# Mixer and MoE block on one core: Y's norm moved ahead of the result's statistics on VectorE, and sixteen repeated products on TensorE before the last group's Y

## The chip, the core and the metric

The kernel runs on one core of a Trainium2 chip. The core's engines each work through a program of their own and meet only at semaphores: TensorE (PE in the profile, its weight loads PEld) multiplies, VectorE (DVE), ScalarE (ACT) and GpSimd (POOL) work elementwise, and SyncE (SP) issues the transfers. Products land in PSUM, which is eight banks here, `bank[0]` to `bank[7]`, of 512 columns each. The metric is the device time of one execution in microseconds (us); lower is better. TensorE's clock has two levels, 1.2 and 2.4 GHz; the profile gives the granted clock of a stretch as a share of the upper one.

## What is computed

An input x of 8 sequences of 1024 tokens with 128 features goes through a recurrent mixer with four heads, a residual sum and a norm; the result, called Y in the kernel, goes through a mixture of experts (16 experts, the best 4 of each token, and a shared one), a residual sum and a norm again:

```python
x = _layernorm(x + mixer(x, ...), axis=-1)            # Y in the kernel
x = _layernorm(x + moe(x, ...), axis=-1)              # z2, then the output

def _layernorm(x, axis=-1, eps=1e-05):
    m = jnp.mean(x, axis=axis, keepdims=True)
    v = jnp.var(x, axis=axis, keepdims=True)
    return (x - m) / jnp.sqrt(v + eps)

# moe, on all tokens xf:
g = sigmoid(xf @ gate_w.T)
topv, topi = top_k(g, 4);  wn = topv / sum(topv);  combine = scatter of wn
h = silu(xf @ e_win) * (xf @ e_vin) * combine          # per expert
out = sum over experts of h @ e_wout  +  silu(xf @ ws_in) * (xf @ vs_in) @ ws_out
```

## The kernel before

A first phase (to about 134 us in the trace) projects, convolves and computes the gates of all tokens and leaves what the mixer needs in DRAM. The second phase is the one that matters here. It goes over 16 groups g of 512 tokens (NG = 16, four chunks of 128 tokens each), and pairs the mixer of group g with the expert part of group f = g - 1, so that every engine's program alternates between the two. `groups` (line 319) sets this: `mix(0, None)`, then a loop over g = 1 to 14 with `mix(g, g - 1)`, then `mix(15, 14)`, and at the end `ffn(15)`, the expert part of the last group alone. The order on each engine is written out by hand; no scheduler changes it.

On TensorE, `mix(g, f)` (line 1410) begins with the transposes of Y (`ffn_head`, line 1348, which wait for `Y_done`), then the key transposes (`key_tokens`, line 1293, which wait for `val_out[1]`, VectorE's copy of the values), the routing logits (line 1354) and eleven slots j. A slot holds six products of 512 columns (`ffn_in`, lines 1366 to 1370: twice hi by hi, lo by hi and hi by lo parts, into `bank[4]` and `bank[5]`), a row product (line 1385), the output products (line 1395) and, in some slots, pieces of the mixer: the chunks of the recurrence (`chunk`, lines 1313 to 1320; chunk k waits for `state_done[k - 1]`), the head transposes (line 1329) and the down projection (line 1339). Last comes `mix_front(g + 1)`: keys, values and scores of the next group (lines 1258, 1267, 1284).

VectorE's `mix(g, f)` (line 1020) ends with what this change touches. `mixer_out` adds the residual (line 1008, `y1`) and takes the statistics of y1 (lines 990 to 998). `ffn_sum` adds the expert output in `bank[7]` to the Y of group f, which is `z2` (line 1105), and takes the statistics of z2. `mixer_norm` writes the new Y over the old one (line 1002), once GpSimd has made `rs1`, the reciprocal root, by one power operation (`power`, line 552). Then come `mix_front(g + 1)` (the values, line 925, and two score products, line 934), `yT_low` (line 1046), and `ffn_norm` (line 1002 again, this time z2 into `out_sb`, which waits for `rs2`). In the next round VectorE goes on with the keys (line 940), the routing (lines 1055 to 1086), the product h of slot 0 (line 1097), and the two sums of `state` after chunk 0 (line 951).

GpSimd makes `rs1`, then `rs2` (line 552 both), and after these, for the next group, `kept` (line 567) and `mixed` (line 573, x times the skip weights, 512 columns from SBUF into SBUF). Later it computes the score masks `D` from `max_b` (line 538), which SyncE loads. SyncE's queue holds, in this order for each group: the store of `out_sb` (line 475, after `out_done`), `x_res`, then the loads of `max_b` (line 404), `xT2` and `inter_w` of the next group.

ScalarE copies the transposed Y out of `bank[7]` twice (`yT` and `yT_hi`, through the helper on line 619), takes the exponential of the logits (line 743) and the silu of each slot (line 754).

The statistics (line 988) are three steps, and each waits for the one before:

```python
for k in range(NC): i = dve.bn_stats(st[:, k], src[:, k])        # line 990
for k in range(NC): i = dve.bn_aggr(mv[:, k], st[:, k])          # line 995
dve.tensor_scalar(ve[:], mv[:, :, 1], EPS_LN, None, ALU.add)     # line 998
```

## Time and profile before

| | us |
|---|---|
| median of 3 runs (lowest, highest) | 866.17 (864.02, 871.2) |
| the profiled execution: its own time | 864.57 |
| its span, first to last instruction | 862.8 |
| mean granted TensorE clock in it | 0.963 |

| engine | busy us | share of the span |
|---|---|---|
| PE | 787.7 | 91% |
| PEld | 666.1 | 77% |
| DVE | 644.4 | 75% |
| ACT | 363.7 | 42% |
| POOL | 371.7 | 43% |

1.8 us of the execution's time lie around the span. The sixteen sums y1 begin between 170.9 and 816.8 us, so one group takes 43.06 us on average; the last expert part alone takes the time from 822 us to the end. Busy shares are averages over the whole span; a matmul's end is modelled, so that the distance between the starts of two of them is the better measure of what one costs. In the timelines a row can hold several instructions of one kind (x4), with the time from the first's start to the last's end; brackets hold the idle time of the engine before the row and what ended it.

### The profile page before, as it was taken

Reading aid. Unit: us, or ns where it says so; the run is one execution under the profiler, and the core shown is the slowest. Engines: PE = TensorE matmul, PEld = TensorE weight load, DVE = VectorE, ACT = ScalarE, POOL = GpSimd, SP = SyncE. Lnnn points to the kernel's source line nnn. Section 1 sums busy time; section 2 is a strip of 40 time slices with the busy share of each in tenths; the row PEclk is TensorE's granted clock in tenths of the full one; section 3 lists DMA queues with packets and bytes.
Section 4 is the critical chain, followed back from the end, with each engine's and each line's share of the span. In section 5 each row is a group of like instructions: output and inputs, shape, how many; then the busy total and the mean of one; then the engine's idle time right before and its main releaser. Section 6 shows DMA issues by size and latency. Waiting matters only on the chain.

```text
span 862.8 us, 17647 instructions
## 1 busy us (share of the span) xinstructions
PE 787.7 (91%) x5783; PEld 666.1 (77%) x5783; DVE 644.4 (75%) x1711; ACT 363.7 (42%) x621; POOL 371.7 (43%) x370
## 2 busy tenths in 40 slices
PE   6888968689999999999999999999999999999976
PEld 5656656578888888888888798888898888888855
DVE  5799953377778777777777877777878777778754
ACT  4757833143434343434343434343434343434131
POOL 5050008553455455454545544545455454543200
PEclk8999977599999999999999999999999999999979
DMA  4887744030404040404040405040404040400000
GB/s 121 237 259 262 288 177 127 30 123 25 135 24 134 24 134 24 134 24 134 24 132 26 134 24 132 26 133 25 134 24 134 24 134 24 134 24 25 1 13 13
DMA packets 53104, 81.01 MB, mean 94 GB/s; under 512 B 10176, under 2 KB 36952, under 8 KB 49112
## 3 DMA queue, kind: packets, MB, share of 16 engines
q1 hardware_dynamic: 53080, 80.68, 30.4%
q8 instruction: 16, 0.26, 0.1%
q14 instruction: 8, 0.07, 0.0%
HBM read 55.24 MB, written 25.43 MB: 93 GB/s over the span
## 4 chain that ended last, share of the span: by engine, by line
PE 45%; DVE 19%; issue 15%; DMA 9%; POOL 6%; ACT 2%; SPq 2%; POOLq 1%; DVEq 1%; ACTq 0%
PE bank L1395 11%; DMA max_b<-max_scratch 8%; PE bank L1366 5%; PE bank L1370 5%; PE bank L1367 5%; DVE acc L838 5%; PE bank L1339 3%; DVE st L990 3%; PE bank L1315 3%; PE bank L1385 3%; PE bank L1313 2%; PE bank L1320 2%; DVE Y L1002 2%; POOL D L548 2%; POOL D L538 2%
## 5 line engine op out<-in xcount | busy, mean ns | idle before, releaser
L754 ACT ACTIVATE s_in<-bank 128x512 f32<-128x512 f32 x144 | 86.1, 598 | 175.9 <-PE bank L1370 174.8
L1395 PEld LDWEIGHTS bank<-ewout,h 128*128 128x128 f32 x1024 | 132.8, 191 | 8.5
L1366 PE MATMUL bank<-yT_hi,in_hi 128*128 128x512 f32 x288 | 128.0, 444 | 8.3 <-DVE h L1097 8.3
L1395 PE MATMUL bank<-ewout,h 128*128 128x128 f32 x1024 | 134.9, 275 | 0.0
L1097 DVE TENSOR_TENSOR h<-s_in,bank 128x512 f32<-128x512 f32 x144 | 98.2, 682 | 49.0 <-PE bank L1370 42.2
L552 POOL TENSOR_TENSOR rs<-ve,half 128x4 f32<-128x4 f32 x32 | 32.6, 1019 | 206.6 <-DVE ve L998 206.6
L1370 PE MATMUL bank<-yT_lo,in_hi 128*128 128x512 f32 x288 | 114.3, 397 | 0.0
L1367 PE MATMUL bank<-yT_hi,in_lo 128*128 128x512 f32 x288 | 113.9, 395 | 0.0
L538 POOL TENSOR_TENSOR D<-a_tok,max_b 128x512 f32<-128x512 f32 x64 | 65.4, 1043 | 110.7 <-DVE max_b L910 67.8
L1101 DVE TENSOR_TENSOR h<-h,bank 128x512 f32<-128x512 f32 x128 | 87.2, 681 | 14.4 <-PE bank L1385 14.4
L951 DVE TENSOR_TENSOR state<-kept,bank 64x130 f32<-64x130 f32 x128 | 36.6, 286 | 59.1 <-PE bank L1320 29.6
L619 ACT ACTIVATE u_sb<-bank 128x260 f32<-128x260 f32 x64 | 24.8, 388 | 131.1 <-PE bank L1315 131.1
L567 POOL TENSOR_TENSOR kept<-state,decay 128x260 f32<-128x260 f32 x64 | 39.7, 620 | 89.0 <-DVE state L951 88.8
L1315 PE MATMUL bank<-vals,C 128*128 128x65 f32 x512 | 73.9, 269 | 0.0
L1366 PEld LDWEIGHTS bank<-yT_hi,in_hi 128*128 128x128 f32 x288 | 55.1, 191 | 20.9 <-DVE h L1097 15.2
L1315 PEld LDWEIGHTS bank<-vals,C 128*128 128x128 f32 x512 | 70.5, 199 | 0.0
L580 POOL TENSOR_TENSOR r_h<-var_h,half 128x8 f32<-128x8 f32 x32 | 52.9, 1653 | 40.2 <-DVE var_h L971 39.1
L838 DVE SCALAR_TENSOR_TENSOR acc<-xm,vecs,acc 128x512 f32<-128x512 f32 x96 | 68.2, 780 | 0.0
L1370 PEld LDWEIGHTS bank<-yT_lo,in_hi 128*128 128x128 f32 x288 | 54.6, 190 | 12.9
L1313 PE MATMUL bank<-state,qs 128*128 128x130 f32 x256 | 56.6, 304 | 7.5 <-issue 5.2
L1367 PEld LDWEIGHTS bank<-yT_hi,in_lo 128*128 128x128 f32 x288 | 55.4, 192 | 5.3
L1313 PEld LDWEIGHTS bank<-state,qs 128*128 128x128 f32 x256 | 41.2, 197 | 16.5 <-issue 15.3
(193 smaller groups left out, 1623.6 us busy)
## 6 DMA issues: line engine op xcount, KB each, us to landing
xact_scratch<-xact SPq DMA_DIRECT2D x16, 1024.0 KB, 4.8
max_b<-max_scratch SPq DMA_DIRECT2D x15, 1024.0 KB, 7.8
xa<-xact_scratch SPq DMA_DIRECT2D x16, 512.0 KB, 6.2
silu_z<-xact_scratch SPq DMA_DIRECT2D x16, 512.0 KB, 3.8
inter_w<-inter_scratch SPq DMA_DIRECT2D x30, 256.0 KB, 7.1
x_in<-in_L_attn_x_dram SPq DMA_DIRECT2D x16, 256.0 KB, 4.8
xt_scratch<-x_t SPq DMA_DIRECT2D x16, 256.0 KB, 4.9
xT<-xt_scratch SPq DMA_DIRECT2D x16, 256.0 KB, 8.2
```

Source lines behind the costliest of these rows:

```text
L538: pool.tensor_tensor(D[:, kp, par], a_g.rearrange("p k (s two) -> p two k s", two=2)[:, par, 2 * kp:2 * kp + 2] .unsqueeze(3).to_broadcast ...
L580: pool.tensor_tensor(r_h[:, c].rearrange("p k h -> p (k h)"), var_h[:, c].rearrange("p k h -> p (k h)"), half[:, 0:2 * NH], ALU.pow).then_ ...
L754: act.activation(s_in[:, j % 2], bank[4][:], ACT.Silu).then_inc(silu_done, 1)
L838: i = dve.scalar_tensor_tensor(a, src, vecs[:, p, t:t + 1], a, ALU.mult, ALU.add)
L1097: dve.tensor_tensor(dst[:, j % 2], s_in[:, j % 2], bank[5][:], ALU.mult).then_inc(h1_done, 1)
L1101: dve.tensor_tensor(h2[:, (j - 1) % 2], h1[:, (j - 1) % 2], bank[6][:], ALU.mult).then_inc(h2_done, 1)
L1313: pe.matmul(o, qs[:, p, c], state[:, p], start=True, stop=False, skip_group_check=True)
L1315: i = pe.matmul(o[:, par * DV:(par + 1) * DV], C[:, par, kk, p], vals[:, k, 2 * p + par], start=False, stop=True, skip_group_check=True)
L1366: pe.matmul(o, in_hi[:, m, j], yT_hi[:], start=True, stop=False)
L1367: pe.matmul(o, in_lo[:, m, j], yT_hi[:], start=False, stop=False)
L1370: pe.matmul(o, in_hi[:, m, j], yT_lo[:], start=False, stop=True).then_inc(done, 1)
L1395: i = pe.matmul(bank[7][:, k * P:(k + 1) * P], h2[:, j % 2, k * P:(k + 1) * P], w, start=(j == k == 0), stop=(j == NJ), skip_group_check=True)
```

## The change

VectorE: `ffn_sum` keeps only the sum z2; its statistics are now `ffn_statistics`, called behind `mixer_norm`. `mixer_norm` waits for the sum z2 as well, since it overwrites the Y that the sum reads. `ffn(15)` calls both parts one after the other, as before. TensorE: `ffn`, which runs once, for the last group, begins with `stay_warm`, which waits for the last silu of the group before and issues 16 products of 512 columns into `bank[4]`; `ffn_in` of slot 0 overwrites them.

```diff
             def mixer_norm(g):
                 dve.wait_ge(rs1_done, g + 1)
+                dve.wait_ge(z2_done, g + 1)
                 normalise(Y, y1, mv1, rs1, Y_done)
@@ VectorE's mix(g, f)
                 mixer_norm(g)
+                if f is not None:
+                    ffn_statistics(f)
                 if not (isinstance(g, int) and g == NG - 1):
                     mix_front(g + 1)
@@
             def ffn_sum(f):
                 dve.wait_ge(o_mm, f + 1)
                 dve.tensor_tensor(flat(z2), bank[7][:], flat(Y), ALU.add).then_inc(z2_done, 1)
+
+            def ffn_statistics(f):
                 dve.wait_ge(z2_done, f + 2)
                 statistics(f, z2, st2, mv2, ve2, st2_done, mv2_done, ve2_done)
@@ VectorE's ffn(f)
                 ffn_sum(f)
+                ffn_statistics(f)
                 ffn_norm(f)
@@ TensorE
+            def stay_warm(f):
+                pe.wait_ge(silu_done, (f + 1) * (NJ + 1))
+                for i in range(WARM):
+                    pe.matmul(bank[4][:], in_hi[:, 0, 0], yT_hi[:], start=True, stop=True)
+
             def ffn(f):
+                stay_warm(f - 1)
                 ffn_head(f)
@@
+WARM = 16
```

VectorE's program in the loop over g = 1 to 14, at the end of `mix(g, g - 1)`. Before:

```order
L998 TENSOR_SCALAR ve<-mv 128x4
L1105 TENSOR_TENSOR z<-bank,Y 128x512
L990 BN_STATS st<-z 128x6 x4
L995 BN_AGGR mv<-st 128x2 x4
L998 TENSOR_SCALAR ve<-mv 128x4
L1002 TENSOR_SCALAR Y<-y,mv,rs 128x128 x4
L924 REGISTER_ALU
L925 COPY vals<-bank 128x8x64
```

Of the change:

```order
L998 TENSOR_SCALAR ve<-mv 128x4
L1108 TENSOR_TENSOR z<-bank,Y 128x512
L1002 TENSOR_SCALAR Y<-y,mv,rs 128x128 x4
L990 BN_STATS st<-z 128x6 x4
L995 BN_AGGR mv<-st 128x2 x4
L998 TENSOR_SCALAR ve<-mv 128x4
L924 REGISTER_ALU
L925 COPY vals<-bank 128x8x64
```

The norm of Y stands ahead of the nine instructions of z2's statistics, and behind the sum z2 in both; the copy of the values follows both in either program.

TensorE's program where the last group's expert part begins, behind the last output products of `mix(15, 14)`. Before:

```order
L1385 MATMUL bank<-combT,pair_rows 128x512
L1395 MATMUL bank<-ewout,h 128x128 x4
L1339 MATMUL bank<-w_down,mixed 128x128 x4
L1395 MATMUL bank<-ewout,h 128x128 x4
L1348 MATMUL bank<-ident,Y 128x128 x4
L1354 MATMUL bank<-w_gate,yT 128x16 x4
```

Of the change, whose lines below 1013 are numbered a few higher:

```order
L1391 MATMUL bank<-combT,pair_rows 128x512
L1401 MATMUL bank<-ewout,h 128x128 x4
L1345 MATMUL bank<-w_down,mixed 128x128 x4
L1401 MATMUL bank<-ewout,h 128x128 x4
L1435 MATMUL bank<-yT_hi,in_hi 128x512 x16
L1354 MATMUL bank<-ident,Y 128x128 x4
L1360 MATMUL bank<-w_gate,yT 128x16 x4
```

Sixteen products stand between the last output products and the transposes of the last Y; nothing else moved on TensorE. The programs of ScalarE, GpSimd and SyncE are the same.

## Rows read from the trace of the kernel before

**Rows 1.** Timeline of PE where group 8 ends and 9 begins: start us, us, instruction, [idle before].
```profile
522.88 0.66 PE L1348 MATMUL bank<-ident,Y 128*128 128x128 f32 x4 [0.34 <-DVE Y L1002]
523.48 0.66 PE L1293 MATMUL bank<-ident,keyT 128*128 128x128 f32 x4
...
529.54 0.40 PE L1370 MATMUL bank<-yT_lo,in_hi 128*128 128x512 f32 x1
530.15 0.46 PE L1313 MATMUL bank<-state,qs 128*128 128x130 f32 x2 [0.21 <-issue]
```

**Rows 2.** Timeline of DVE at the same boundary.
```profile
517.14 0.69 DVE L1008 TENSOR_TENSOR y<-bank,x_res 128x512 f32<-128x512 f32 x1 [1.10 <-PE bank L1339]
517.87 0.87 DVE L990 BATCH_NORM_STATS2 st<-y 128x6 f32<-128x128 f32 x4
...
519.38 0.68 DVE L1105 TENSOR_TENSOR z<-bank,Y 128x512 f32<-128x512 f32 x1
520.10 0.87 DVE L990 BATCH_NORM_STATS2 st<-z 128x6 f32<-128x128 f32 x4
...
521.72 1.11 DVE L1002 TENSOR_SCALAR Y<-y,mv,rs 128x128 f32<-128x128 f32 x4
522.74 0.69 DVE L925 COPY vals<-bank 128x512 f32<-128x512 f32 x1
523.34 1.28 DVE L934 TENSOR_TENSOR C<-bank,D 128x512 f32<-128x512 f32 x2
524.69 0.69 DVE L1046 TENSOR_TENSOR yT_lo<-bank,yT_hi 128x512 fp32r<-128x512 f32 x1
525.30 1.11 DVE L1002 TENSOR_SCALAR out_sb<-z,mv,rs 128x128 f32<-128x128 f32 x4
...
529.47 0.58 DVE L951 TENSOR_TENSOR state<-kept,bank 64x130 f32<-64x130 f32 x2
```

**Rows 3.** Timeline of POOL, then of ACT, at the same boundary.
```profile
519.55 1.01 POOL L552 TENSOR_TENSOR rs<-ve,half 128x4 f32<-128x4 f32 x1 [9.39 <-DVE ve L998]
521.89 1.03 POOL L552 TENSOR_TENSOR rs<-ve,half 128x4 f32<-128x4 f32 x1 [1.33 <-DVE ve L998]
522.89 0.62 POOL L567 TENSOR_TENSOR kept<-state,decay 128x260 f32<-128x260 f32 x1
523.49 1.56 POOL L573 TENSOR_SCALAR mixed<-xa,vecs 128x512 f32<-128x512 f32 x1
...
524.07 0.59 ACT L619 ACTIVATE yT_hi<-bank 128x512 fp32r<-128x512 f32 x1
```

**Rows 4.** Timeline of POOL and DVE behind group 0, without an expert part.
```profile
174.28 0.62 POOL L567 TENSOR_TENSOR kept<-state,decay 128x260 f32<-128x260 f32 x1
174.88 1.57 POOL L573 TENSOR_SCALAR mixed<-xa,vecs 128x512 f32<-128x512 f32 x1
...
174.35 2.18 DVE L1002 TENSOR_SCALAR Y<-y,mv,rs 128x128 f32<-128x128 f32 x4 [1.12 <-POOL rs L552]
```

**Rows 5.** Timelines of SP and POOL: the store, and the masks that wait for max_b.
```profile
526.58 0.41 SPq L475 DMA_DIRECT2D out_dram<-out_sb  x1
...
535.86 2.04 POOL L538 TENSOR_TENSOR D<-a_tok,max_b 128x512 f32<-128x512 f32 x2 [3.40 <-DMA max_b<-max_scratch]
```

**Rows 6.** Timelines of PE, DVE and ACT at the start of the last expert part.
```profile
816.65 1.06 PE L1395 MATMUL bank<-ewout,h 128*128 128x128 f32 x8
822.57 1.12 PE L1348 MATMUL bank<-ident,Y 128*128 128x128 f32 x4 [4.87 <-DVE Y L1002]
...
833.12 1.03 PE L1376 MATMUL bank<-ident,comb 128*32 128x128 f32 x4 [2.29 <-DVE comb L1086]
...
829.12 0.69 DVE L1097 TENSOR_TENSOR h<-s_in,bank 128x512 f32<-128x512 f32 x1 [1.78 <-PE bank L1370]
...
826.30 0.22 ACT L743 ACTIVATE ge<-bank 128x64 f32<-128x64 f32 x1 [0.19 <-PE bank L1354]
...
827.84 0.60 ACT L754 ACTIVATE s_in<-bank 128x512 f32<-128x512 f32 x1
```

**Rows 7.** Busy time by stretch: window: its length, PE, PEld, DVE, ACT, POOL, PEclk, DMA.
```profile
820.00:822.00 2.00, 0.00 (x0) 0.00 (x0) 1.82 (x12) 0.00 (x0) 0.78 (x2) 1.00 0.00 0
822.00:824.00 2.00, 1.12 (x4) 0.72 (x4) 0.52 (x3) 0.28 (x1) 0.61 (x1) 0.62 0.00 0
...
834.00:836.00 2.00, 2.00 (x6) 1.60 (x6) 0.00 (x0) 1.12 (x2) 0.00 (x0) 0.50 0.00 0
```

## The prediction

> **What bounds the kernel now.** I read the timelines of all engines around one boundary between two groups, since the change moves VectorE's work there, and then the start of the last expert part, where TensorE's new products stand. The fifteen later boundaries repeat within a few hundredths of a microsecond, so one stands for the fourteen in the loop over g = 1 to 14.
>
> At the boundary the time first passes from TensorE to VectorE: the sum y1 starts at 517.14, after a wait of 1.10 us for the down projection [rows 2]. TensorE then has the next group's front to do and needs Y only at the end of it: it waits 0.34 us for Y, starts the transposes at 522.88, and is nearly dense until 529.54 [rows 1]. Its next product, chunk 1, starts at 530.15. Products of 512 columns start 0.23 us apart here when nothing waits, so it could have started at about 529.77; what it waited for is `state`, whose two sums on VectorE run from 529.47 to 530.05 [rows 1, 2]. So both paths meet at chunk 1, and VectorE's is the later one, by 0.38 us. That path has almost no idle time: from 517.14 to 530.05 each row of VectorE starts when the one ahead of it lets it [rows 2]. It is therefore VectorE's work and not TensorE's wait for Y that sets when chunk 1 starts, and with it the rest of the group, in which TensorE is mostly dense.
>
> A second chain leaves from the same place. The store of `out_sb` is issued at 526.58, right behind the norm into `out_sb` (525.30 plus 1.11), and the load of `max_b` is queued behind it; GpSimd waits 3.40 us for that load and starts the masks at 535.86 [rows 2, 5]. Whatever delays `out_sb` delays this as well, so that neither chain can take up a slip of the other.
>
> **The change, step by step, in the loop (14 times).**
>
> 1. *Y's norm.* The sum z2 keeps its place, from 519.38 to 520.06. The norm needs `rs1`, which GpSimd makes from 519.55 to 520.56 [rows 2, 3]. A norm that waited for `rs1` started some 0.04 us behind it [rows 4], so it starts at 520.60 in place of 521.72: Y comes 1.12 us earlier. TensorE's wait of 0.34 us for Y goes. It can't take more: it is still at its scores until 522.54. And the key transposes behind (523.48 now) wait for the copy of the values, which comes later, below.
>
> 2. *What VectorE loses.* Before, z2's statistics started at 520.10 and covered the time in which `rs1` was made. Now VectorE stands still from 520.06 to 520.60. Then the four norms take 1.02 us (521.72 to 522.74, start to start), and the statistics 1.51 (517.87 to 519.38, those of y1) to 1.62 (520.10 to 521.72, those of z2) [rows 2]. The copy of the values starts at 520.60 + 1.02 + 1.51 to 1.62 = 523.13 to 523.24 in place of 522.74: a slip of 0.45 us, give or take 0.05.
>
> 3. *Up to `out_sb`.* The two score products follow with 0.60 us each after the copy. `yT_lo` waited 0.14 us for ScalarE's `yT_hi`: the second score product was issued at about 523.95, the next could have started at 524.55, it started at 524.69, and `yT_hi` ended at 524.66 [rows 2, 3]. `yT_hi` comes 0.34 us earlier now, with the transposes. That takes 0.14 off the slip. The norm into `out_sb` starts 0.31 us late, at 525.61.
>
> 4. *GpSimd meets VectorE.* z2's statistics end later, so `rs2` starts at about 523.37 (the value copy's new start, less 0.08 for the overlap with the last statistics step, plus its 0.17 and a start 0.08 behind it) in place of 521.89. `kept` and `mixed` are queued behind `rs2` and slip with it by 1.48 us: `mixed` ran from 523.49 to 525.05, just clear of `out_sb` at 525.30, and now runs from 524.97 to 526.53 [rows 3]. The norm into `out_sb` lies in it for 526.53 - 525.61 = 0.92 us. Behind group 0 the trace shows the same pair together: four norms take 2.18 us while GpSimd runs `kept` and `mixed`, against the 1.11 of both norms at the later boundary [rows 2, 4]. That is 1.07 us lost in 2.10 us of overlap (174.35 to 176.45), 0.51 per us. So 0.92 us of overlap costs 0.47 us. The ends of this term: nothing, if the phase is lucky, and 0.92, if VectorE stands still for all of it.
>
> The Trainium skill has a rule for this pair (the page "SBUF — State Buffer", section "SBUF: two separate sides"): VectorE and GpSimd share one pair of ports, held by one of them for a whole instruction, and the loser "fully blocks". By it the term would be 0.92. The trace agrees that there is a collision but not with a full block, since under it the four norms behind group 0 could not all have ended 0.08 us behind `mixed`.
>
> Sum for one boundary: 0.31 + 0.47 = 0.78 us later at `state`. TensorE gets to chunk 1 later by that, as its own path has not slipped as far (the key transposes wait for the copy of the values, 523.9 in place of 523.48, and the transposes of Y ahead of them left 0.34 us earlier; I put it at 0.2 to 0.4 us, inside the 0.38 us in hand plus 0.78). `mixed` and `kept` themselves are needed only at 529.47, so their slip costs nothing but the collision. 14 x 0.78 = 10.9 us. Bounds: 14 x 0.31 = 4.3 and 14 x 1.23 = 17.2.
>
> **The change at the end (once).**
>
> 5. *Y.* TensorE stands still for 4.87 us before the last transposes at 822.57 [rows 6]. The norm moves forward by 1.12 us as above, and nothing else is behind it here: 1.1 us gained.
>
> 6. *The sixteen products.* TensorE's last output products started at 816.65 and ended at 817.71; sixteen at 0.23 us are 3.7 us, from about 817.6 to 821.3, and the transposes can start at 821.45. So they lie wholly in the wait, with 0.1 us to spare, and cost nothing; at 0.25 us each or more they would begin to push the transposes, by 0.3 us for each 0.02. In their place the engine was idle, and its granted clock was 1.00 until 822, then 0.62 on average over the next 2 us, that is, it fell to the lower level within them [rows 7]. The transposes took 1.12 us against 0.66 in the loop [rows 1, 6]. I expect it to stay up. The silu of slot 0 started at 827.84 behind `ge`, which had waited 0.19 for the logits; with 0.46 from the transposes and these 0.19 the silu comes 0.65 earlier and ends 5.22 us behind the transposes' start. The product h of slot 0 started at 829.12, 6.55 behind it, held by TensorE's slow products; now it follows the silu: 1.3 us gained. Everything of the routing is queued behind that h, up to the combine transposes (833.12) [rows 6].
>
> 7. *The second fall.* There the clock is low again (0.50 from 834 to 836) [rows 7], after a wait of 2.29 us [rows 6]. That wait remains, at about 2.4 us, so I count nothing. If the clock holds, up to about 3 us at the lower level become 1.5: at most 1.5 gained; if it falls sooner, as much is lost.
>
> Sum at the end: 1.1 + 1.3 = 2.4 us gained, from 1.0 to 3.9.
>
> **Net.** +10.9 - 2.4 = +8.5 us. On the profiled execution's own time that is 864.57 + 8.5 = 873.1; that execution lies 1.6 us under the median of the runs, from which the same sum gives 874.7. I say 874.
>
> **Rivals.**
>
> *A. No collision.* `out_sb` and `mixed` alternate without loss, as one norm of the pair can slip through where GpSimd isn't at the memory. Then 4.3 - 2.4 = +1.9: 868. For it: the score products and `yT_lo` run at their usual time beside `kept` and `mixed` [rows 2, 3]. Against it: the norm has already been caught once [rows 4].
>
> *B. A full block.* 17.2 - 2.4 = +14.8: 881. It is what the lock would do, worked from `mixed`'s new end at 526.53; the full 1.07 of group 0 per boundary would end at much the same place.
>
> *C. TensorE's path decides (faster).* If chunk 1 isn't held by `state` but by something on TensorE's own path, then Y's 0.34 us comes off each boundary: 14 x 0.34 = 4.8, and with the 2.4 at the end -7.2: 859. This holds only if VectorE has at least 0.78 us in hand between the copy of the values and `state`; the rows show no gap of that size, and a wait of 0.38 us on the other side [rows 1, 2].
>
> *D. The products don't hold the clock.* They are the same product sixteen times, and the clock falls at 822 anyway. Then only Y's 1.1 us remain at the end: 10.9 - 1.1 = +9.8: 875.5 to 876. Against it: the level was 1.00 for the whole loop, in which TensorE did nothing else than such products.
>
> **How the numbers follow.** The forecast (collision at half rate, clock held) gets 0.45 with a range of its own of 870 to 878; A 0.17, B 0.18, C 0.10, D 0.10. The predicted time is 874. From 864 to 881 leaves out most of C, and the upper part of B, together under 2 in 10. About 1% (8.7 us) is what a measurement of this kernel can tell from no change. Faster by more than that (under 857.5) needs C and a kind tail: 0.05. Slower by more (over 874.8) takes B, most of D and nearly half of the forecast: 0.43. Within 1%: 0.52.
>
> **What would show it.** In the timeline of the changed kernel: the norm of Y 3.46 us behind the sum y1 instead of 4.58, with an idle of about 0.5 us before it put down to `rs`; the copy of the values 6.05 behind y1 in place of 5.60 (step 2); the norms into `out_sb` at 1.4 to 2 us for four instead of 1.11 (step 4); chunk 1 about 13.8 us behind y1 in place of 13.0, and the distance of two sums y1 0.8 us above 43.06 on average. At the end, a granted clock of 1.00 from 820 to the first ffn products, and combine transposes 2.4 us sooner behind y1 (about 16.3 now). I am wrong if chunk 1 does not move: then VectorE had slack that I didn't see. I am wrong in size if `out_sb` keeps its 1.11 us.

## The result, and the profile after

| | before | changed | |
|---|---|---|---|
| median of the runs, us (runs) | 867.04 (20) | 871.85 (20) | ratio 1.0079, 95% interval 1.0058 to 1.0100 |
| lowest, highest | 861.29, 874.61 | 866.30, 878.19 | |
| span of the profiled execution | 862.8 | 864.6 | |
| its granted TensorE clock | 0.963 | 0.973 | |

The changed kernel is 0.8% slower: by the ratio 6.8 us, from 5.0 to 8.8. The two medians lie only 4.8 us apart (the means 4.3), just under that interval, so the size of the whole is less certain than its sign. The two profiled executions differ by only 1.8 us, since the first phase happened to be 3.5 us shorter in the later one (the first sum y1 at 167.4 against 170.9). What the change touches lies behind that, and is best read as distances from the sums y1 (line 1008), one per group:

| us | before | changed |
|---|---|---|
| between two sums y1, mean over the loop (14) | 43.07 | 43.58 |
| the same, shortest | 42.11 | 42.59 |
| norm of Y behind y1 | 4.57 | 3.45 |
| copy of the values behind y1 | 5.60 | 6.01 |
| state (chunk 0) behind y1 | 12.32 | 12.76 |
| TensorE's chunk 1 behind y1 | 13.01 | 13.44 |
| at the end: combine transposes behind the last y1 | 16.27 | 14.19 |
| at the end: last instruction of VectorE behind the last y1 | 43.26 | 41.38 |

The loop lost 7.2 us (14 x 0.51) and the end gained 1.9, as these two executions show it.

The mean distance of two sums y1 needs care, since what ends a group is not the same in all 14. In 9 of them in the trace of the kernel before, and in 10 in that of the changed kernel, the next y1 stands 24.3 us behind the start of GpSimd's masks, however late they start: these groups end by the masks, and the masks wait for `max_b`. At 42.11 to 42.13 (4 groups), and at 42.59 and 42.61 (2 groups), `state` decides; in the rest (1 and 2 groups) the masks meet the routing, as the section on the transfers shows. Here is the load of `max_b` at the boundary of group 8, first before, then changed (SPq is SyncE's queue):

```profile
528.09 0.35 SPq L404 DMA_DIRECT2D max_b<-max_scratch  x1
```

```profile
525.60 0.35 SPq L404 DMA_DIRECT2D max_b<-max_scratch  x1
```

It is issued 10.95 us behind y1 before and 11.38 in the changed kernel, as `out_sb`, whose store stands ahead of it, is late by as much. So the groups that end by the masks are moved by 0.43 us on this way. The time from issue to landing is between 4.8 and 8.5 us in one trace, 4.8 and 8.7 in the other (medians 7.8 and 7.6, between 250 and 820 us), and scatters the mean distance of an execution; the shortest distance is free of that. Here is VectorE at the boundary of group 8 in the changed kernel, which answers to [rows 2]; its y1 stands at 514.22 where it stood at 517.14.

```profile
514.22 0.69 DVE L1008 TENSOR_TENSOR y<-bank,x_res 128x512 f32<-128x512 f32 x1 [1.10 <-PE bank L1345]
...
516.46 0.68 DVE L1108 TENSOR_TENSOR z<-bank,Y 128x512 f32<-128x512 f32 x1
517.67 1.12 DVE L1002 TENSOR_SCALAR Y<-y,mv,rs 128x128 f32<-128x128 f32 x4 [0.53 <-POOL rs L552]
518.70 0.86 DVE L990 BATCH_NORM_STATS2 st<-z 128x6 f32<-128x128 f32 x4
...
520.23 0.69 DVE L925 COPY vals<-bank 128x512 f32<-128x512 f32 x1
520.84 1.28 DVE L934 TENSOR_TENSOR C<-bank,D 128x512 f32<-128x512 f32 x2
522.03 0.68 DVE L1049 TENSOR_TENSOR yT_lo<-bank,yT_hi 128x512 fp32r<-128x512 f32 x1
522.63 1.29 DVE L1002 TENSOR_SCALAR out_sb<-z,mv,rs 128x128 f32<-128x128 f32 x4
...
526.98 0.58 DVE L951 TENSOR_TENSOR state<-kept,bank 64x130 f32<-64x130 f32 x2
```

The norm waits 0.53 us for `rs`, a wait that wasn't there; the statistics stand behind it and cover nothing. `out_sb` takes 1.29 us where it took 1.11. GpSimd and TensorE at the same place (for [rows 3] and [rows 1]):

```profile
520.38 1.01 POOL L552 TENSOR_TENSOR rs<-ve,half 128x4 f32<-128x4 f32 x1 [2.75 <-DVE ve L998]
521.36 0.62 POOL L567 TENSOR_TENSOR kept<-state,decay 128x260 f32<-128x260 f32 x1
521.96 1.57 POOL L573 TENSOR_SCALAR mixed<-xa,vecs 128x512 f32<-128x512 f32 x1
```

```profile
519.54 0.66 PE L1354 MATMUL bank<-ident,Y 128*128 128x128 f32 x4
520.98 0.66 PE L1299 MATMUL bank<-ident,keyT 128*128 128x128 f32 x4 [0.78 <-DVE vals L925]
...
526.73 0.40 PE L1376 MATMUL bank<-yT_lo,in_hi 128*128 128x512 f32 x1
527.66 0.46 PE L1319 MATMUL bank<-state,qs 128*128 128x130 f32 x2 [0.53 <-issue]
```

`mixed` runs from 521.96 to 523.53, over the norm at 522.63 to 523.92. TensorE no longer waits for Y but waits 0.78 us for the values right behind it, and its gap ahead of chunk 1 is 0.93 from start to start where it was 0.61. So Y's earlier arrival was exchanged for a later copy of the values on the engine that decides.

At the end (for [rows 6] and [rows 7]):

```profile
820.28 1.06 PE L1401 MATMUL bank<-ewout,h 128*128 128x128 f32 x8
821.09 3.93 PE L1435 MATMUL bank<-yT_hi,in_hi 128*128 128x512 f32 x16
825.42 0.66 PE L1354 MATMUL bank<-ident,Y 128*128 128x128 f32 x4 [0.40 <-DVE Y L1002]
...
834.67 0.86 PE L1382 MATMUL bank<-ident,comb 128*32 128x128 f32 x4 [1.98 <-DVE comb L1089]
```

```profile
820.00:828.00 8.00, 6.91 (x42) 5.62 (x42) 5.97 (x26) 1.87 (x3) 2.01 (x2) 1.00 0.00 1
828.00:832.00 4.00, 3.56 (x10) 2.37 (x9) 2.88 (x13) 2.60 (x4) 0.00 (x0) 0.57 0.22 66
832.00:834.00 2.00, 0.69 (x4) 0.22 (x2) 1.86 (x13) 0.60 (x1) 0.00 (x0) 1.00 0.00 0
834.00:838.00 4.00, 3.33 (x11) 2.67 (x12) 0.58 (x3) 1.18 (x2) 0.00 (x0) 0.61 0.00 0
```

The second list gives each stretch's length, the busy time of PE, PEld, DVE, ACT and POOL, then the granted clock. The sixteen products fill the wait and the clock stays at 1.00 through it and through the transposes, which take 0.66 us (1.12 before). It falls to the lower level only at about 828, and again at about 835.

### The profile page after: what moved, and what is told of

Its sections match the earlier page's. It is cut to its first block, busy times and chain, and to the rows that moved or that the text cites. A ratio compares the mean times of both kernels' runs of the same rounds, so it can differ in the third digit from the quotient of the medians.

```text
span 864.6 us, 17695 instructions
## 1 busy us (share of the span) xinstructions
PE 783.3 (91%) x5799; PEld 661.2 (76%) x5799; DVE 648.9 (75%) x1711; ACT 364.3 (42%) x621; POOL 371.6 (43%) x370
## 4 chain that ended last, share of the span: by engine, by line
PE 44%; DVE 20%; issue 15%; DMA 9%; POOL 7%; SPq 3%; DVEq 1%; POOLq 1%; ACT 1%; ACTq 0%
PE bank L1401 11%; DMA max_b<-max_scratch 9%; PE bank L1372 6%; PE bank L1376 5%; PE bank L1373 5%; DVE acc L838 5%; PE bank L1345 3%; DVE st L990 3%; PE bank L1391 3%; PE bank L1321 3%; DVE Y L1002 2%; POOL rs L552 2%; PE bank L1319 2%; PE bank L1326 2%; PE bank L1335 2%
## 5 line engine op out<-in xcount | busy, mean ns | idle before, releaser
L1321 PE MATMUL bank<-vals,C 128*128 128x65 f32 x512 | 72.0, 264 | 0.0
L1321 PEld LDWEIGHTS bank<-vals,C 128*128 128x128 f32 x512 | 68.3, 194 | 0.0
```

The lines of the kernel that those rows point to most:

```text
L1321: i = pe.matmul(o[:, par * DV:(par + 1) * DV], C[:, par, kk, p], vals[:, k, 2 * p + par], start=False, stop=True, skip_group_check=True)
```

## The experiments

Theory: the loop is slower because VectorE's path from y1 to `state` sets when chunk 1 starts, and the change lengthens it twice, by the idle for `rs1` and by the collision of `out_sb` with `mixed`; the end is faster by the earlier Y and by the clock. The rivals: TensorE's own program or path, the transfers (`max_b` is queued behind `out_sb`), or an end that gains only by Y. All ratios below are to the kernel before, each with its 95% interval. The distances are medians over the boundaries in the loop.

| kernel | ratio | state behind y1 | shortest distance of two y1 | its mean | combine transposes, last | last VectorE instruction |
|---|---|---|---|---|---|---|
| before | 1 | 12.32 | 42.11 | 43.07 | 16.27 | 43.26 |
| changed | 1.0079 (1.0058 to 1.0100) | 12.76 | 42.59 | 43.58 | 14.19 | 41.38 |
| e1_order_only | 1.0075 (1.0037 to 1.0114) | 12.76 | 42.55 | 43.64 | 15.48 | 42.49 |
| e2_warm_only | 1.0006 (0.9972 to 1.0039) | 12.32 | 42.11 | 43.35 | 15.15 | 42.52 |
| e3_last_only | 0.9974 (0.9940 to 1.0009) | 12.25 | 42.04 | 43.13 | 14.19 | 41.37 |
| e4_hold_mixed | 1.0004 (0.9969 to 1.0039) | 12.58 | 42.37 | 43.54 | 14.19 | 41.40 |
| e5_slip | 1.0036 (1.0007 to 1.0065) | 12.64 | 42.44 | 43.67 | 16.45 | 42.06 |
| e7_split_hold | 0.9882 (0.9848 to 0.9916) | 11.91 | 41.70 | 43.15 | 14.20 | 41.41 |
| e9_fill_after | 1.0059 (1.0035 to 1.0083) | 12.78 | 42.57 | 43.68 | 14.20 | 39.80 |
| e10_max_early | 0.9951 (0.9917 to 0.9986) | 12.33 | 43.04 | 43.02 | 15.87 | 43.04 |
| e12_after_max_early | 0.9974 (0.9944 to 1.0004) | 12.77 | 43.49 | 43.43 | 14.19 | 41.36 |
| e13_early_held | 0.9818 (0.9783 to 0.9853) | 12.33 | 42.11 | 42.14 | 16.11 | 43.31 |
| e14_after_early_held | 0.9825 (0.9796 to 0.9853) | 12.78 | 42.57 | 42.58 | 14.20 | 41.37 |
| e11_all | 0.9683 (0.9651 to 0.9715) | 11.91 | 41.70 | 41.73 | 14.19 | 39.77 |

For e10 and e12 the shortest is that of the loop's distances apart from the last, which has no masks to make for a next group (42.15 and 42.57).

### The two parts alone, and the order only at the end

**e1_order_only**, against the changed kernel:

```diff
             def ffn(f):
-                stay_warm(f - 1)
                 ffn_head(f)
```

> The changed kernel without the sixteen repeated products: only the new order on VectorE. Theory (the order costs 0.44 us per boundary through VectorE's path to state, the products gain at the end): the two state sums 12.77 us behind the sum y1 in the loop as in the changed kernel (12.33 before), TensorE's last transposes 4.6 us behind y1 (5.72 before), the clock low from about there on as before, combine transposes about 15.1 us behind y1 (16.27 before, 14.19 in the changed kernel). Whole time +5 to +7 us against the kernel before, about 1 us slower than the changed kernel. Rival (the products themselves cost time, or do nothing): combine transposes at 14.2 or sooner without them.

**e2_warm_only** is the kernel before with `stay_warm` and nothing else of the change.

> The kernel before with the sixteen repeated products alone, the order on VectorE unchanged. Theory: loop as before (chunk 0 to state 12.33 us behind y1); at the end the transposes stay 5.72 us behind y1, the granted clock stays at 1.00 over the wait, and the combine transposes come 15.3 us behind y1 in place of 16.27: whole time -1 us, 866. Rival (the gain at the end came from the earlier Y alone): combine transposes at 16.2.

**e3_last_only**, against the changed kernel:

```diff
+                late = isinstance(g, int) and g == NG - 1
+                if f is not None and not late:
+                    ffn_statistics(f)
                 mixer_norm(g)
-                if f is not None:
+                if late:
                     ffn_statistics(f)
```

> The changed kernel with the new order only behind the last mixer group (g = 15), the old order at the fourteen boundaries in the loop; the sixteen products stay. Theory (the loss sits in the loop, the gain at the end): state 12.33 us behind y1 in the loop, combine transposes 14.2 us behind y1 at the end, whole time -2 us against the kernel before and 7 to 9 us under the changed kernel. Rival (the loss is not VectorE's order but comes from elsewhere, such as TensorE's program or the transfers): the loop stays at 43.5 us per group.

The loss goes with the order in the loop. With the order alone the loop is as slow as in the changed kernel (state at 12.76, shortest distance 42.55) and the whole is 1.0075; with the order at the end only, the loop is back (42.04) and the end keeps all it gained (14.19), for 0.9974. The products alone bring the combine transposes from 16.27 to 15.15, the order alone to 15.48, both together to 14.19: the two gains nearly add up there, 1.12 and 0.79 against 2.08. At VectorE's last instruction they don't: 0.74 and 0.77 against 1.88. The whole time of e2 can't tell its gain from nothing; only the trace does.

The mean distances agree with the shortest ones once several traces are taken together. The three with the old order in the loop and `max_b` as it was (before, e2, e3) have 43.07, 43.35 and 43.13, the three with the new order (changed, e1, e9) 43.58, 43.64 and 43.68: 0.45 us apart on average.

The end of the kernel before isn't a fixed number. e5, e10 and e13 below have its program there (e5 with one memset more on VectorE), and their combine transposes come at 16.45, 15.87 and 16.11, their last instruction at 42.06, 43.04 and 43.31, since the clock falls and rises at other moments. Here are the kernel before and e5 in like stretches, 17.2 and 16.5 us behind the last y1 (granted clock 0.73 and 1.00):

```profile
834.00:838.00 4.00, 4.00 (x19) 3.33 (x19) 1.29 (x2) 1.19 (x2) 0.00 (x0) 0.73 0.00 0
```

```profile
842.00:846.00 4.00, 4.00 (x24) 3.49 (x25) 1.28 (x2) 1.40 (x3) 0.00 (x0) 1.00 0.00 0
```

All six kernels that have the changed end, without e9's additions, lie between 41.36 and 41.41. So the change gains 0.7 to 1.9 us at the end, 1.5 against the mean of the four unchanged ends; and e2's 42.52 lies within the range of the unchanged ends, so that only at the combine transposes (15.15 against 15.87 at the least) is the gain of the products alone clear.

### The collision

**e4_hold_mixed**, against the changed kernel, in GpSimd's `mix`:

```diff
                         prev(pool, down_mm, g)
+                        pool.wait_ge(keytok_out[0], g + 1)
                         alone(pool)
```

> The changed kernel, and GpSimd's first mixed of a group waits until VectorE has written keys, so that it no longer runs beside the norm into out_sb. Theory (0.18 of the 0.44 us per boundary is that collision): the four norms take 1.11 us again instead of 1.29, state comes 12.59 us behind y1, and the whole is 2.5 us faster than the changed kernel (14 x 0.18). Rival (the norms are slower for another reason, or something waits for mixed): the norms stay at 1.29, or state stays at 12.77.

The groups by line of VectorE between 250 and 820 us, first of the kernel before, then of the changed kernel, then of e4 (busy us, mean ns of one, idle before and its releaser):

```profile
L1002 DVE TENSOR_SCALAR out_sb<-z,mv,rs 128x128 f32<-128x128 f32 x52 | 14.4, 340 | 0.0
```

```profile
L1002 DVE TENSOR_SCALAR out_sb<-z,mv,rs 128x128 f32<-128x128 f32 x52 | 16.8, 479 | 0.0
L1002 DVE TENSOR_SCALAR Y<-y,mv,rs 128x128 f32<-128x128 f32 x52 | 14.5, 343 | 6.9 <-POOL rs L552 6.9
```

```profile
L1003 DVE TENSOR_SCALAR out_sb<-z,mv,rs 128x128 f32<-128x128 f32 x52 | 14.4, 338 | 0.0
```

With `mixed` out of the way the norms are at 340 ns again and state comes 0.18 us sooner, as expected; the shortest distance falls from 42.59 to 42.37. The collision is shown, and its price: 0.18 us per boundary. The whole time fell by more than the 2.5 us that this makes (1.0004 against 1.0079, some 6 us, with an interval of about 3 us on e4's ratio alone; by the medians, each against its own kernel before, 4.2 us). The mean distance in its profile, 43.54, doesn't show that excess, so I don't claim it.

### Does VectorE's path set the time?

**e5_slip**, against the kernel before:

```diff
                 mixer_norm(g)
+                if f is not None:
+                    dve.memset(slip[:], 0.0)
                 if not (isinstance(g, int) and g == NG - 1):
                     mix_front(g + 1)
```

> The kernel before with one added instruction on VectorE at each of the fifteen boundaries with an expert part, between the norm of Y and the copy of the values: a memset of 512 columns that nothing reads or waits for. It slips VectorE's path without touching the order, Y, GpSimd's place or the end. Theory (VectorE's path from y1 to state sets the period): state and the start of chunk 1 slip by the instruction's own length less 0.14 us (the wait for yT_hi takes that up), and the periods with it; with 0.3 to 0.55 us per memset that is 14 times 0.2 to 0.4, 2 to 6 us. Rival (VectorE has slack there, and the changed kernel is slower for another reason): chunk 1 stays 13.0 us behind y1 and the shortest period at 42.1.

```profile
L1040 DVE MEMSET slip<- 128x512 f32 x13 | 6.3, 485 | 0.7
```

The memset takes 0.49 us, state slips by 0.32, chunk 1 by 0.32 (13.32) and the shortest distance by 0.33. The score products slip by 0.49 and `yT_lo` by 0.33: the slack ahead of it took up 0.16, where I had counted 0.14. Y, the order and GpSimd's part stayed as they were, and the whole is slower, 1.0036, where 14 x 0.33 = 4.6 us would be 1.0053, inside the interval. VectorE has no slack there; in the groups that end by the masks the slip passes on through `out_sb` and `max_b`. The faster outcome would have needed it.

### Without the idle

**e7_split_hold**, against the changed kernel (with e4's wait as well): of z2's statistics the first step goes ahead of the norm, the rest behind it.

```diff
             def ffn_stats(f):
                 dve.wait_ge(z2_done, f + 2)
                 for k in range(NC):
                     i = dve.bn_stats(st2[:, k], z2[:, k])
                 i.then_inc(st2_done, 1)
@@ mix(g, f); ffn_aggr(f) holds the other two steps
-                mixer_norm(g)
-                if f is not None:
-                    ffn_statistics(f)
+                late = isinstance(g, int) and g == NG - 1
+                if f is not None and not late:
+                    ffn_stats(f)
+                mixer_norm(g)
+                if late:
+                    ffn_stats(f)
+                if f is not None:
+                    ffn_aggr(f)
```

> The changed kernel with two edits: in the loop only the first step of z2's statistics (four instructions on line 990, 0.87 us) stays ahead of Y's norm, so that it covers the making of rs1, and the rest follows the norm; and GpSimd's first mixed waits for the keys. Theory (the loss of the changed kernel is VectorE's idle of 0.5 us plus the collision of 0.18): the idle is gone and the norm starts 3.8 us behind y1, the values are copied 5.3 us behind y1 (5.6 before, 6.01 in the changed kernel), state comes about 12.05 us behind it (12.33, 12.77), the shortest period is 41.85 (42.11, 42.59): 6 us under the kernel before, 861. Rival (TensorE's own path sets chunk 1 once VectorE is faster): state comes sooner but chunk 1 stays at 12.9 or later, whole time 864 to 865.

State comes at 11.91, 0.85 sooner than in the changed kernel and 0.41 sooner than before, chunk 1 at 12.59, and the shortest distance is 41.70. TensorE's path was not yet the bound. The idle for `rs1` was therefore the larger part of the loss: 0.26 us of slip at `out_sb` (8.16 to 8.42 behind y1), against 0.18 for the collision.

That it is sooner than before, too, has a reason that the rows show. The second step of z2's statistics waited 0.25 us for the first in the kernel before (the first line); in e7 the norm stands between them and this idle time is gone (the other two):

```profile
521.22 0.38 DVE L995 BATCH_NORM_AGGREGATE mv<-st 128x2 f32<-128x6 f32 x4 [0.25 <-DVE st L990]
```

```profile
520.28 1.10 DVE L1003 TENSOR_SCALAR Y<-y,mv,rs 128x128 f32<-128x128 f32 x4
521.29 0.37 DVE L1126 BATCH_NORM_AGGREGATE mv<-st 128x2 f32<-128x6 f32 x4
```

The whole is 0.9882, some 10 us, more than the 6 expected. The profile doesn't show the excess: its mean distance is 43.15, and 11 of its 14 groups end by the masks. It stays open.

### The transfers

The rival that the loss comes through the late `max_b` needed a kernel in which the transfer is not late.

**e10_max_early**, against the kernel before, and **e12_after_max_early**, the same against the changed kernel, in SyncE's queue (the first load now stands ahead of the first group, and the last rounds are written out to fit):

```diff
-                sp.wait_ge(arg_sub, nth(g, 4, 3))
                 if not (isinstance(g, int) and g == NG - 1):
-                    load_max(g + 1)
                     sp.wait_ge(val_mm[1], g + 1)
...
                     load_z(g + 1)
+                if not (isinstance(g, int) and g >= NG - 2):
+                    sp.wait_ge(arg_sub, nth(g + 1, 4, 3))
+                    load_max(g + 2)
                 if f is not None:
                     store(f)
```

> The kernel before with the load of max_b issued one place earlier in the transfer queue: behind the load of silu_z and ahead of the store of out_sb, instead of behind the store. Theory (the periods above the shortest, 42.11, are all groups in which GpSimd's masks wait for max_b and chunk 3 waits for them): GpSimd no longer waits for max_b, all periods in the loop become 42.1 in place of 43.1 on average, whole time 13 us less, 853. Rival (the long periods come from contention of the transfers or of memory and not from the place in the queue): periods stay spread from 42.1 to 44 and the time within 3 us of before.

> The changed kernel with the load of max_b issued earlier in the same way, so that the spread of the periods is gone and the change's cost can be read against the kernel before with that same edit. Theory: all periods 42.55 to 42.6 against 42.1, so 14 x 0.46 = 6.4 us slower in the loop, 2 us faster at the end, 4 to 4.5 us slower as a whole. Rival (part of the loss comes through the transfers, because out_sb and with it max_b are late): less than 0.3 us per period is left, and the two are within 2 us.

The first expectation failed, and usefully. The wait for `max_b` went, and the spread with it, but the distances settled at 43.06 and not at 42.1. (The whole is 0.9951 all the same, with its interval under 1; the distances of its one profile, 43.02 on average against 43.07, 43.35 and 43.13 in the three traces with late loads, show only a part of this.) In e10's groups by line, against those of the kernel before, the two last routing steps stand out; first before, then e10:

```profile
L1086 DVE TENSOR_TENSOR comb<-comb 128x64 fp32r<-128x64 f32 x13 | 4.1, 316 | 0.4
L1084 DVE CAST comb<-comb 128x64 fp32r<-128x64 f32 x13 | 2.5, 196 | 0.4
```

```profile
L1094 DVE TENSOR_TENSOR comb<-comb 128x64 fp32r<-128x64 f32 x13 | 12.5, 961 | 0.4
L1092 DVE CAST comb<-comb 128x64 fp32r<-128x64 f32 x13 | 8.5, 655 | 0.4
```

and in its timelines, TensorE waits for them while GpSimd makes the masks:

```profile
534.00 2.04 POOL L546 TENSOR_TENSOR D<-a_tok,max_b 128x512 f32<-128x512 f32 x2
...
534.39 0.70 DVE L1092 CAST comb<-comb 128x64 fp32r<-128x64 f32 x1
535.12 1.00 DVE L1094 TENSOR_TENSOR comb<-comb 128x64 fp32r<-128x64 f32 x1
...
536.18 0.61 PE L1384 MATMUL bank<-ident,comb 128*32 128x128 f32 x4 [0.76 <-DVE comb L1094]
```

The masks came early enough to meet the routing, and averages of 0.20 and 0.32 us became 0.66 and 0.96 (the second step is 0.23 us in 11 of its 13 rows before, and 1.10 in the one group in which the masks met it there too). For the change itself the pair answers cleanly: without a late transfer the distances are 43.50 against 43.06, 0.44 us apart, the same as the slip of state. The medians of the two whole times are 4.5 us apart. So a late transfer adds nothing to the loss: it only takes the same slip to the end of the group on another way.

**e13_early_held** and **e14_after_early_held** add to these a wait in GpSimd, ahead of the first masks of a group (and `args` is now called with f):

```diff
                 if kp == 0:
+                    if f is not None:
+                        pool.wait_ge(route, (f + 1) * ROUTE)
+                        alone(pool)
                     pool.wait_ge(max_in, 16 * (g + 1))
```

> The kernel before with max_b loaded early as in the last run but one, and GpSimd's masks held until VectorE has finished the routing's last step. With max_b early alone the masks began 15.3 us behind y1, beside the two routing steps on lines 1084 and 1086 (0.70 and 1.00 us there, 0.20 and 0.22 in the kernel before), and every period was 43.06. Theory (the transfer is late in half the groups, and where it isn't, the collision costs as much): held, all periods in the loop are 42.1, 13 us under the kernel before, 855. Rival (the masks have to start at 15.3 for the rest to be in time): periods stay at 43.

> The changed kernel with both edits of e13_early_held, to read the change against it without spread. Theory: all periods 42.55 against 42.1, 14 x 0.44 = 6.2 us slower in the loop, 1.8 faster at the end: 4.4 us slower than e13_early_held as a whole. Rival: as before, less than 0.3 us per period.

Now all distances are 42.14 and 42.58: 14 x 0.44 = 6.2 us of loss in the loop, and 43.31 against 41.37, 1.9 us of gain at the end. That makes 4.3 us. The two ratios, 0.9818 and 0.9825, are only 0.6 us apart with intervals of 3 us each. Taken directly, the means of the six and six times on one chip differ by 0.8 us, and an interval worked out from their scatter goes from -2 to 3.5, which leaves 4.3 out; for e12 against e10 (twelve and twelve) it goes from 2.7 to 7.4. The loss in the loop is shown by every distance; what becomes of it in the whole time of this pair stays open. Both kernels are some 15 us faster than the kernel before.

### The clock at the end

**e9_fill_after**, against the changed kernel, in the last expert part; `bank[1]` is free there, and the sixteen products of `stay_warm` now write it too, through `repeat`:

```diff
+            def repeat(n):
+                for i in range(n):
+                    pe.matmul(bank[1][:], in_hi[:, 0, 0], in_hi[:, 0, 0:4], start=True, stop=True)
             def ffn(f):
                 stay_warm(f - 1)
                 ffn_head(f)
+                repeat(3)
                 ffn_logits(f)
                 for j in range(NJ + 3):
+                    if j == 1:
+                        repeat(6)
+                    elif j == 2:
+                        repeat(8)
                     ffn_slot(f, j)
```

> The changed kernel with more repeated products in the last expert part, into a bank that is free there: 3 behind the transposes of Y, 6 ahead of slot 1 and 8 ahead of slot 2, where TensorE waits. In the changed kernel the clock still falls twice there, at 828.1 (behind the transposes and logits) and again at about 834.9, and is low until 831.5 and 838.3. Theory (TensorE's own idle and thin stretches bring the clock down): it stays at 1.00 to the end, the combine transposes stay near 14.2 us behind y1 (the routing on VectorE holds them), and the last instruction comes 1.4 to 1.6 us sooner behind y1 (41.38 in the changed kernel, 39.8 to 40.0 here). Rival (repeated products don't hold the clock, or cost as much as they give): 41.0 or more.

The granted clock of e9 in the stretches that were low in the changed kernel (its last y1 is 3.6 us later), and in between:

```profile
832.00:834.00 2.00, 2.00 (x11) 1.56 (x9) 1.40 (x5) 1.96 (x4) 0.00 (x0) 1.00 0.11 33
834.00:836.00 2.00, 2.00 (x9) 1.31 (x8) 1.47 (x12) 0.88 (x2) 0.00 (x0) 1.00 0.34 98
836.00:838.00 2.00, 1.84 (x9) 1.17 (x7) 1.86 (x11) 0.00 (x0) 0.00 (x0) 1.00 0.00 0
838.00:840.00 2.00, 1.69 (x10) 1.43 (x11) 0.23 (x1) 0.93 (x2) 0.00 (x0) 1.00 0.00 0
840.00:842.00 2.00, 2.00 (x15) 1.79 (x14) 1.29 (x2) 0.26 (x1) 0.00 (x0) 1.00 0.00 0
```

The clock stays at 1.00, the combine transposes stay where they were (14.20), and the last instruction comes 1.58 us sooner (39.80). So the second fall was worth 1.6 us, and products that nothing reads can hold the clock.

The first fall is another matter. e4, e7 and e14 have the changed kernel's program on TensorE in the last expert part, without e9's products, and there the clock stayed up where it fell in the changed kernel, e3 and e12, and fell only the second time. e4, with its last y1 at 822.63:

```profile
830.00:834.00 4.00, 2.61 (x11) 1.73 (x11) 2.94 (x13) 2.90 (x5) 0.10 (x1) 1.00 0.22 66
...
838.00:842.00 4.00, 4.00 (x16) 3.53 (x15) 1.29 (x2) 0.65 (x2) 0.00 (x0) 0.58 0.00 0
```

So e9 doesn't show that its three products behind the transposes prevented the first fall, and that fall cost nothing at the end: the last instruction comes at 41.38, 41.37 and 41.36 with it, and at 41.40, 41.41 and 41.37 without. The second fall came in all six, and in neither of the two kernels with products in the waits (e9 and e11).

### All of it

**e11_all** has e7's split, e4's wait, e13's two edits and e9's products.

> What the runs point to, in one kernel: the statistics of z2 split around Y's norm and GpSimd's first mixed held (as in e7_split_hold), max_b loaded early with the masks held (as in e13_early_held), and the repeated products in all of TensorE's waits of the last expert part (as in e9_fill_after). Theory: periods 41.70 in the loop (43.07 before), 14 x 1.37 = 19.2 us, and 3.4 us at the end: 22 us under the kernel before, about 845, faster than either kernel. Rival (the gains overlap, since another path comes up once these are gone): periods at 42.1 and 850 or more.

The distances are 41.73 throughout and the ratio is 0.9683: 839.08 us against 867.79 for the kernel before on the same chip. The gains did not overlap. The 28.7 us between these medians are more than the 22 of the theory; 18.8 of them are the loop (14 x 1.34), 1.7 are the first boundary (41.26 against 42.98), 3.5 the end, and the remaining 5 I can't place from one profile of each. In these two profiled executions the first phase, which no edit touches, is shorter by 4.4 us (first y1 at 166.5 and 170.9) and makes up the difference; whether it does so in the medians, nothing shows. Over all the profiles that first y1 lies between 166.5 and 174.9.

## Why the prediction was right, step by step

It gave 874 with a range of 864 to 881; the measured median is 871.85, and against its own median the forecast was +8 us, the measured ratio +6.8 (4.8 by the two medians).

*What bounds the kernel*: right. The two paths meet at chunk 1 and VectorE's is the later one; a slip put on it alone slips chunk 1 and the distances (e5), and taking time off it brings them in (e7). But "with it the rest of the group" holds only for the groups that don't end by the masks, 4 of the 14. The boundary that I read belongs to the others: its masks waited 3.40 us for `max_b`, and its next y1 stands 43.06 us on. The prediction named that second chain and said that it slips alike, and so it did (10.95 to 11.38 behind y1), which is why the sum could still be taken 14 times.

*Step 1, Y's norm*: right. It starts 3.45 behind y1 (3.46 foretold), and the transposes 5.32.

*Step 2, VectorE's loss*: right. The values are copied 6.01 behind y1; 6.05 was the sum.

*Step 3, up to `out_sb`*: right, 0.26 in place of 0.31, since the copy of the values slipped by 0.41 and not by 0.45; the slack ahead of `yT_lo` took up 0.15.

*Step 4, the collision*: the mechanism was right and the term was too large: 0.18 us per boundary in place of 0.47. `mixed` lay over the norms for 0.90 us, as foretold. What failed was the rate of 0.51 us lost per us of overlap, taken from group 0. There the norms met `kept` and all of `mixed`, and took 635, 737, 336 and 709 ns; here they met only the last 0.90 us of `mixed`. The four norms at 522.63 took 335, 722, 532 and 328 ns: two were held, two ran at their usual length, the first of them wholly beside `mixed`. In both places the loss is not spread evenly over GpSimd's instruction, so a mean rate can't be carried over; what decides which norm is held, no run here shows. The rule of the Trainium skill ("SBUF — State Buffer", "SBUF: two separate sides") that the loser fully blocks for the whole instruction would have made it 0.92; the trace disagrees here too, since the first norm ran at full speed within `mixed`, and all four had ended 0.39 us behind its end (523.92 against 523.53). The same page of the Trainium skill, in the same section, also says that only some of VectorE's instructions use the shared pair, those in a two-port mode and those with two inputs in SBUF. With that the trace agrees: the score products and `yT_lo`, which read PSUM, took 0.67 to 0.69 us in every kernel, beside `kept` and `mixed` or not.

*TensorE's own slip*, which I put at 0.2 to 0.4 us, was 0.12; it stayed covered by `state` as foretold.

*Sum for one boundary*: 0.44 in place of 0.78, so 6.2 us in the loop in place of 10.9.

*Step 5, Y at the end*: 0.79 in place of 1.12. The sum z2 itself started 0.2 us later there (2.55 behind y1 against 2.33), after a pause of 0.20 us inside y1's own statistics, which the profile puts down to nothing. The late z2 is there in every kernel with the norm moved, and in e5 too (2.52); I didn't find its cause.

*Step 6, the products*: right in what they cost (nothing: the transposes still wait 0.40 us for Y) and right in that the clock holds over the wait. h of slot 0 came 5.26 behind the transposes in place of 6.55, 1.3 us gained as foretold. That it would then stay up was not foretold, and it fell at 828.

*Step 7, the second fall*: it remained, and cost 0.2 us more than before (2.08 gained at the combine transposes, 1.88 at the last instruction), in this pair of traces. e9 shows that it is worth 1.6 us in all, where I gave at most 1.5.

*The sum at the end*: 1.9 in place of 2.4, and 1.5 against the mean of the four unchanged ends. *Net*: 6.2 - 1.9 = 4.3 by the pieces, or 5.3 with the mean distances of the two profiles, against 6.8 (5.0 to 8.8) by the ratio and 4.8 by the medians. That the forecast of 8.5 lies near the ratio is luck in part: its loop was too large by 4.7 us, of which 4.1 (14 x 0.29) are the collision.

## What to carry to other kernels

Before work is moved ahead of other work on a busy engine, ask what the work that stood between was covering: here z2's statistics hid the making of `rs1` on another engine, and putting the norm first turned them into idle time plus the same statistics. Only as much as the wait is long should stay in between (e7). An engine that waits for a result isn't helped by having it sooner if the next thing that it needs comes later from the same engine.

When a transfer or a step is made earlier, look at what it will now run beside: `max_b` early left the mean distance of the groups where it was (43.02 against 43.07) until the masks were held behind the routing (42.14).

## What the runs showed of the hardware

The meeting of VectorE and GpSimd was dearer elsewhere than in the change itself. A routing step with two SBUF inputs of 64 columns took 0.23 us alone and 0.96 on average beside GpSimd's masks, and a cast of 64 columns 0.20 and 0.66; neither kernel's busy shares hint at it, and it moved every group by 0.92 us (e10 against e13).

Sixteen repeats of one product, whose result nothing reads, kept the granted clock at 1.00 (2.4 GHz) over a wait in which it fell to the lower level (1.2 GHz) without them; it held in all nine profiles with them and fell in all five without. Behind the wait the same program did not always get the same clock. In the changed kernel, e3 and e12 it fell 7 to 8 us behind the last y1 (828 in the changed kernel), while TensorE was not idle: behind it lay four transposes, a wait of 0.69 us and the logit products of 16 columns. In e4, e7 and e14 it did not fall there, with the same products in the same order. What decides between the two, no run here separates; so the end of this kernel has to be read from several traces.
